# Seeding PSUM banks from ScalarE: D times xc, the mixer's residual and the convolution's last tap

## The reference

```python
xb, z = split(rms_norm(x) @ in_proj_w)
xc = silu(conv1d(xb, conv_w, 4 taps, causal, per channel) + conv_b)
dt, B, C = split(xc @ x_proj_w); dt = softplus(dt @ dt_proj_w + dt_proj_b)
h = exp(dt * A) * h + dt * B * xc          # a scan over the 1024 tokens
y = sum over states of h * C
y = (y + xc * D) * silu(z)
out = y @ out_proj_w + x                   # residual
```

## Time and profile before

| | us |
|---|---|
| median of 3 runs | 2755.98 (2751.46 to 2756.31) |
| the profiled execution's own time | 2754.25 |
| its span, first to last instruction | 2752.5 |
| busy: PE | 2418.8 |
| busy: DVE | 2434.5 |
| busy: ACT | 1633.1 |
| busy: POOL | 1511.1 |

### The profile page before, as it was taken

How to read it: one execution, slowest core, us unless ns; L and a number is a source line. 1 busy time by engine, 2 the same in 40 slices (tenths; PEclk the granted TensorE clock), 3 DMA queues, 4 the chain that set the end, 5 groups by cost and what they waited for, 6 DMA issues and landing times.

```text
span 2752.5 us, 27115 instructions
## 1 busy us (share of the span) xinstructions
PE 2418.8 (88%) x8416; PEld 1183.5 (43%) x8416; DVE 2434.5 (88%) x3233; ACT 1633.1 (59%) x3312; POOL 1511.1 (55%) x548
## 2 busy tenths in 40 slices
PE   4556799998989999998999999898999989888987
PEld 1112254453545444444544445453544545443554
DVE  1699999999999999999999999999999999999532
ACT  3565656666665667566566667666566666644321
POOL 0255565655556565655656565565656555565422
PEclk9777899999999999999999999999999999999999
DMA  1623253534344343524435353443535343442232
GB/s 35 231 86 124 94 177 93 180 118 153 114 134 155 118 158 118 183 87 156 140 115 177 101 176 109 144 137 103 186 93 179 118 155 105 137 157 80 68 87 56
DMA packets 175563, 353.43 MB, mean 128 GB/s; under 512 B 16283, under 2 KB 82108, under 8 KB 166972
## 3 DMA queue, kind: packets, MB, share of 16 engines
q1 hardware_dynamic: 164668, 334.93, 36.3%
q0 software_dynamic: 10752, 16.78, 3.7%
HBM read 291.35 MB, written 51.90 MB: 125 GB/s over the span
## 4 chain that ended last, share of the span: by engine, by line
DVE 57%; issue 19%; ACT 15%; PE 7%; POOL 1%; DMA 1%; DVEq 0%; SPq 0%; POOLq 0%; ACTq 0%
DVE hs L897 26%; DVE hs L883 12%; DVE th L1007 5%; DVE th L1012 4%; ACT DX L529 2%; DVE XC L856 2%; PE Gp L424 2%; ACT dA L511 1%; ACT L511 1%; PE Up L432 1%; PE FP L351 1%; PE FP L361 1%; ACT XC L582 1%; ACT SZ L587 1%; ACT XB L529 1%
## 5 line engine op out<-in xcount | busy, mean ns | idle before, releaser
L782 POOL TENSOR_TENSOR hs<-hs,Cb 128x2048 f32<-128x2048 f32 x256 | 1170.6, 4572 | 199.8 <-DVE hs L883 199.8
L511 ACT ACTIVATE dA<-dtr,A 128x512 f32<-128x512 f32 x1024 | 701.8, 690 | 827.9 <-DVE hs L897 826.9
L762 POOL TENSOR_TENSOR th<-th,cmb 128x512 f32<-128x512 f32 x256 | 338.1, 1325 | 803.4 <-DVE hs L883 711.8
L897 DVE TENSOR_TENSOR_SCAN hs<-dA,carry,hs 128x512 f32<-128x512 f32 x512 | 627.7, 1265 | 19.8 <-ACT dA L511 19.4
L424 PE MATMUL Gp<-x2T,Wgu 128*128 128x512 f32 x1024 | 532.6, 645 | 115.2 <-DVE th L1007 115.1
L897 DVE TENSOR_TENSOR_SCAN hs<-dA,hs 128x512 f32<-128x512 f32 x512 | 596.1, 1203 | 31.6 <-ACT dA L511 31.1
L883 DVE TENSOR_TENSOR hs<-dxr,Bb 128x2048 f32<-128x2048 f32 x256 | 601.9, 2351 | 12.5 <-DMA dxr<-dx_d 12.5
L432 PE MATMUL Up<-x2T,Wgu 128*128 128x512 f32 x1024 | 492.7, 604 | 0.0
L442 PE MATMUL MY<-Wdn,th 128*128 128x256 f32 x2048 | 486.4, 380 | 0.2 <-POOL th L762 0.2
L442 PEld LDWEIGHTS MY<-Wdn,th 128*128 128x128 f32 x2048 | 383.5, 190 | 137.4 <-issue 94.7
L424 PEld LDWEIGHTS Gp<-x2T,Wgu 128*128 128x128 f32 x1024 | 182.2, 196 | 449.5 <-issue 253.6
(11 more groups left out here) (131 smaller groups left out, 1820.5 us busy)
## 6 DMA issues: line engine op xcount, KB each, us to landing
dtr<-dt_d SPq DMA_DIRECT2D x64, 1024.0 KB, 5.7
dxr<-dx_d SPq DMA_DIRECT2D x128, 512.0 KB, 7.5
cmb<-cm_d SPq DMA_DIRECT2D x256, 256.0 KB, 3.7
Wdn<-in_w_dn SPq DMA_DIRECT2D x256, 128.0 KB, 3.6
dt_d<-XB SPq DMA_DIRECT2D x16, 1024.0 KB, 4.3
dx_d<-DX SPq DMA_DIRECT2D x16, 1024.0 KB, 5.9
Bb<-bc_d SPq DMA_DIRECT2D x64, 256.0 KB, 3.0
Cb<-bc_d SPq DMA_DIRECT2D x64, 256.0 KB, 4.0
```

Of the source, the lines that this page charges most:

```text
L511: act.activation(dA[h % 2][:, :], dtr[:, M % 2, beta, :], ACT.Exp, scale=A[:, k:k + 1]).then_inc(s_dA, 1)
L762: pool.tensor_tensor(th[:, q % NTH, :], th[:, q % NTH, :], cmb[:, q % 2, :], ALU.mult).then_inc(m_a, 1)
L782: pool.tensor_tensor(hs[:, G % NH, :, :], hs[:, G % NH, :, :], Cb[:, s, :].unsqueeze(1).broadcast_to([P, NBETA, CH]), ALU.mult).then_inc(s ...
L897: dve.tensor_tensor_scan(hv, dA[h % 2][:, :], hv, first, ALU.mult, ALU.add).then_inc(s_h, 1)
```

## The change

ACT writes three addends into the PSUM banks before PE adds its products:

- `y_begin`, new, heads ACT's groups g = 2, 6, 10, 14. It waits for `silu_x` and `y_gate` and writes D times xc into `Y` (new semaphore `y_seed`). `add_states` waits for `y_seed`; its `Ddiag` matmul is gone.
- After `f_b` of blocks 2 and 3, ACT rewrites `FP` in place as last tap times value plus bias (steps `seed2`, `seed3`). `f_conv` adds three taps to it without a bank of its own; `f_tap` becomes a plain copy.
- `p_xn` writes into `FP`, not `rn`, and moves: half 0 to the end of g = 1, half 1 to g = 3 behind `p_rev(0)`. `p_out` adds onto it. The identity matmul is gone. At stages without a front (p = 15, 16) a matmul `p_clear` (fill `rz`, g = 1) comes first. One matmul into `Y` (`y_first`) is added at the start of the program.

The rows of `Y` are now in natural channel order, so the stores permute the channels: each of the two 1 MB stores becomes four of 32 partitions each. The setup no longer builds `Ddiag` (4 DVE instructions) and builds 6 of 8 blocks of `Kdiag`.

```diff
-FREED_BY = dict(..., b2='raw2', b3='raw3', k2='tap2', k3='tap3', ...)
+FREED_BY = dict(rz='xn0', ..., k2='tap2', k3='tap3', ...)
...
-        def channels(t, c):
-            return t.rearrange('(c m p) t -> c p m t', m=MT, p=P)[c]
+        def channels(t, c, b):
+            return t.rearrange('(c m k b) t -> c b k m t', m=MT, k=CB, b=NBETA)[c, b]
...
-                        sp.dma_start(channels(dt_d, c), dt).then_inc(st_dt, 16)
+                        for b in range(NBETA):
+                            sp.dma_start(channels(dt_d, c, b), dt[b * CB:(b + 1) * CB, :, :]).then_inc(st_dt, 16)
...
             pe.wait_ge(w_dve, 2)
+            pe.matmul(Y[:, :], ident, Win[:, 0, 0:CH], start=True, stop=True).then_inc(y_first, 1)
...
             def f_conv(p, m):
-                bank_free(p, f'k{m}')
-                pe.wait_ge(f_act.sem, f_act.at(c, f'raw{m}'))
+                pe.wait_ge(f_act.sem, f_act.at(c, f'seed{m}'))
...
-                for k in range(TAPS):
+                for k in range(HIST):
...
+            def p_clear(p):
+                bank_free(p, 'rz')
+                pe.matmul(FP[:, :], ident, Win[:, 0, 0:CH], start=True, stop=True).then_inc(fp_full, 1)
...
             def p_out(p, k):
-                bank_free(p, f'r{k}')
+                pe.wait_ge(p_act.sem, p_act.at(c, f'xn{k}'))
...
-                    mm = pe.matmul(o, ident, rn[:, b, :], start=False, stop=True)
...
             def add_states(G):
                 if s == 0:
-                    if G > 0:
-                        pe.wait_ge(y_gate, G // NSIG)
-                    pe.wait_ge(f_act.sem, f_act.at(c, 'silu_x'))
-                    pe.matmul(Y[:, :], Ddiag[:, m, :], XC[:, c % 2, m, :], start=True, stop=False)
+                    pe.wait_ge(y_seed, G // NSIG + 1)
...
             def f_b(p, m):
                 act.activation(XB[:, m, HIST:], FP[:, :], ACT.Copy).then_inc(f_act.sem, 1)
+                if m in PE_CONV:
+                    act.activation(FP[:, :], FP[:, :], ACT.Identity, scale=conv_w[:, m, HIST:HIST + 1], bias=conv_b[:, m:m + 1]).then_inc(f_act.sem, 1)
...
+            def y_begin(M):
+                c, m = divmod(M, MT)
+                act.wait_ge(f_act.sem, f_act.at(c, 'silu_x'))
+                if M > 0:
+                    act.wait_ge(y_gate, M)
+                else:
+                    act.wait_ge(y_first, 1)
+                act.activation(Y[:, :], XC[:, c % 2, m, :], ACT.Identity, scale=d_col[:, m:m + 1]).then_inc(y_seed, 1)
...
             for p, g, G in groups():
+                if 0 <= G - 2 < NGRP and g % NSIG == 2:
+                    y_begin((G - 2) // NSIG)
                 if 0 <= p < NC:
                     decay(G * NBETA + 2)
                     decay(G * NBETA + 3)
                 if R_ and g in (3, 4):
                     p_rev(p, g - 3)
+                if R_ and g == 3:
+                    p_xn(p, 1)
...
-                if R_ and g in (0, 1):
-                    p_xn(p, g)
+                if R_ and g == 1:
+                    p_xn(p, 0)
```

More of the change, by code:

```diff
@@ L53, in fills_of @@
 def fills_of(p):
-    return [f for f in FILLS if (in_e(p) if f in E_FILLS else in_p(p) if f in P_FILLS else in_f(p))]
+    return [f for f in FILLS if not (f == 'rz' and in_f(p)) and (in_e(p) if f in E_FILLS else in_p(p) if f in P_FILLS else in_f(p))]
 FILL_NO = {pf: k for k, pf in enumerate([(p, f) for p in range(-2, NC + 1) for f in fills_of(p)])}
@@ L107, in sandwich_kernel @@
         A = sb('A', [P, GPC * NBETA])
-        Ddiag = sb('Ddiag', [P, MT, P])
-        Kdiag = sb('Kdiag', [P, len(PE_CONV) * TAPS, P])
+        Kdiag = sb('Kdiag', [P, len(PE_CONV) * HIST, P])
         Ebias = sb('Ebias', [P, TB * NE])
-        Cst = sb('Cst', [P, P + CB + NG * NG + TB * NE + P])
+        Cst = sb('Cst', [P, P + CB + NG * NG + TB * NE])
         SelDt = sb('SelDt', [2 * NS + 1, P])
@@ L168, in sandwich_kernel @@
         e_act = Steps(sem('e_act'), ['sum', 'nm', 'sq', 'xr'])
-        f_act = Steps(sem('f_act'), ['xT0', 'xT1', 'raw0', 'tap0', 'raw1', 'tap1', 'raw2', 'tap2', 'raw3', 'tap3', 'z0', 'silu_x', 'xd', 'dt', 'z1', 'z2', 'z3', 'silu_z'])
+        f_act = Steps(sem('f_act'), ['xT0', 'xT1', 'raw0', 'tap0', 'raw1', 'tap1', 'raw2', 'seed2', 'tap2', 'raw3', 'seed3', 'tap3', 'z0', 'silu_x', 'xd', 'dt', 'z1', 'z2', 'z3', 'silu_z'])
         f_dve = Steps(sem('f_dve'), [f'c{k}{m}' for m in DVE_CONV for k in range(HIST)] + ['hist', 'dx'])
@@ L172, in sandwich_kernel @@
         s_u, s_dA, s_h, s_keep, s_c, s_y, y_gate = (sem(k) for k in ('s_u', 's_dA', 's_h', 's_keep', 's_c', 's_y', 'y_gate'))
+        y_first, y_seed = (sem('y_first'), sem('y_seed'))
         route = ['den', 'score', 'sfc', 'ps', 't1', 't2', 'gs', 'ggt', 'geq', 'gq', 'ga', 'gr', 'gm', 'tmp', 'top', 'gt', 'eq', 'ng', 'cs', 'cn', 'ok', 'sel', 'w', 'ws', 'we', 'wr', 'comb']
         p_dve = Steps(sem('p_dve'), ['w1', 'nb', 'Bw1'] + rsqrt_names('q') + ['Bnb'] + route)
-        p_act = Steps(sem('p_act'), ['xn0', 'xn1', 'rev0', 'rev1', 'nm', 'sq', 'ro', 'sum2', 'nm2', 'sq2', 'x2', 'x2T0', 'x2T1', 'sig', 'cmT'])
+        p_act = Steps(sem('p_act'), ['xn0', 'rev0', 'xn1', 'rev1', 'nm', 'sq', 'ro', 'sum2', 'nm2', 'sq2', 'x2', 'x2T0', 'x2T1', 'sig', 'cmT'])
         m_g, m_u, m_d, m_th, m_v, m_w, m_a = (sem(k) for k in ('m_g', 'm_u', 'm_d', 'm_th', 'm_v', 'm_w', 'm_a'))
@@ L274, in _ @@
                         sp.wait_ge(f_act.sem, f_act.at(c, 'dt'))
-                        sp.dma_start(channels(dt_d, c), dt).then_inc(st_dt, 16)
+                        for b in range(NBETA):
+                            sp.dma_start(channels(dt_d, c, b), dt[b * CB:(b + 1) * CB, :, :]).then_inc(st_dt, 16)
                     if g == 11:
                         sp.wait_ge(f_dve.sem, f_dve.at(c, 'dx'))
-                        sp.dma_start(channels(dx_d, c), DX[:, :, :]).then_inc(st_dx, 16)
+                        for b in range(NBETA):
+                            sp.dma_start(channels(dx_d, c, b), DX[b * CB:(b + 1) * CB, :, :]).then_inc(st_dx, 16)
                 if in_p(p) and g == 10:
@@ L355, in f_conv @@
                 c = p + 1
-                bank_free(p, f'k{m}')
-                pe.wait_ge(f_act.sem, f_act.at(c, f'raw{m}'))
+                pe.wait_ge(f_act.sem, f_act.at(c, f'seed{m}'))
                 if m == PE_CONV[0] and c > 0:
                     pe.wait_ge(f_dve.sem, f_dve.at(c - 1, 'hist'))
-                for k in range(TAPS):
-                    mm = pe.matmul(FP[:, :], Kdiag[:, PE_CONV.index(m) * TAPS + k, :], XB[:, m, k:k + CH], start=k == 0, stop=k == TAPS - 1)
+                for k in range(HIST):
+                    mm = pe.matmul(FP[:, :], Kdiag[:, PE_CONV.index(m) * HIST + k, :], XB[:, m, k:k + CH], start=False, stop=k == HIST - 1, skip_group_check=True)
                 mm.then_inc(fp_full, 1)
@@ L474, in _ @@
                     f_dt(p)
+                if R_ and not F and g == 1:
+                    p_clear(p)
                 if R_ and g in (2, 3):
@@ L570, in f_tap @@
                     act.wait_ge(s_y, (c - 2) * GPC + m * NSIG + 1)
-                act.activation(XC[:, c % 2, m, :], FP[:, :], ACT.Identity, bias=conv_b[:, m:m + 1]).then_inc(f_act.sem, 1)
+                act.activation(XC[:, c % 2, m, :], FP[:, :], ACT.Copy).then_inc(f_act.sem, 1)
             def f_z(p, m):
@@ L613, in p_xn @@
                     act.wait_ge(e_dve.sem, e_dve.at(c, 'nbr'))
-                    act.wait_ge(st_dx, 16 * min(p + 1, NC))
+                    if in_f(p):
+                        act.wait_ge(f_act.sem, f_act.at(p + 1, 'tap2'))
+                    else:
+                        act.wait_ge(fp_full, filled(p, 'rz'))
+                else:
+                    act.wait_ge(p_act.sem, p_act.at(c, 'rev0'))
                 for b in (2 * k, 2 * k + 1):
-                    ins = act.activation(rn[:, b, :], x1[:, c % 2, b, :], ACT.Identity, scale=ln1[:, c, 0, b:b + 1], bias=ln1[:, c, 1, b:b + 1])
+                    ins = act.activation(FP[:, b % 2 * DM:(b % 2 + 1) * DM], x1[:, c % 2, b, :], ACT.Identity, scale=ln1[:, c, 0, b:b + 1], bias=ln1[:, c, 1, b:b + 1])
                 ins.then_inc(p_act.sem, 1)
@@ L800, in _ @@
                 dve.tensor_scalar(Win[:, q, :], Win[:, q, :], norm_w[:, q:q + 1], None, ALU.mult)
-            for m in range(MT):
-                dve.tensor_scalar(Ddiag[:, m, :], to_y, d_col[:, m:m + 1], None, ALU.mult)
             for m in PE_CONV:
-                for k in range(TAPS):
-                    dve.tensor_scalar(Kdiag[:, PE_CONV.index(m) * TAPS + k, :], ident, conv_w[:, m, k:k + 1], None, ALU.mult)
+                for k in range(HIST):
+                    dve.tensor_scalar(Kdiag[:, PE_CONV.index(m) * HIST + k, :], ident, conv_w[:, m, k:k + 1], None, ALU.mult)
             dve.memset(XB[:, :, 0:HIST], 0.0).then_inc(w_dve, 1)
```

33 lines of the change are left out of this document (15 added, 18 removed).

## The result

The changed kernel takes 2810.59 us (median; 2809.3 to 2812.08), the kernel before 2755.15 beside it: 1.0203 times as long, 95% interval 1.019 to 1.0217. The predicted time was 2808.

A forecast was written before the change was run, and what follows sets the result against it. The prediction took DVE, interrupted where ACT is late, to bound the steady stages. Wait 29 + clock 27 + 0.7 - 1.2 - 0.5 - 0.9 = +54 on 2754.25 gave 2808 us; range 2752 to 2842, 8 times in 10.

The forecast's parts named there:

- The wait: At g = 6 PE's sums wait for ACT's seed, so z0 and DVE's scan in g = 7 come 2.05 us later: 14 x 2.05 = 29 us.
- all but the wait and the clock: Seed at p = 0, setup, the head's convolutions and the tail: + 0.7 - 1.2 - 0.5 - 0.9 us.
- 2 us or more: Sign in the changed profile: ACT idle this long before f_z of z0 in g = 6, released by PE.
- The clock at g = 6: Behind a 3.8 us PE stall, gate and up run partly at 1.2 GHz, z0 2.1 us later: 13 x 2.1 = 27 us.
- The clock at g = 5: Rival: some 3 us idle before gate of g = 5 also brings 1.2 GHz; another 28 us, 2836 us; chance 0.13.
- The head's clock: Rival: y_first and the changed rhythm bring the clock up for the first projections; 7 us back, 2745 us; chance 0.13.
- The seed's own cost: On ACT, 0.65 us per seed of Y and 0.75 per FP; 96 seeds, about 66 us, beside idle time but for one place.
- PE's lighter work: PE loses 141 us, 6% of its work, all beside DVE's work; counted at nothing in the steady stages.
- The edits counted at nothing: y_begin at g = 2, 10, 14, seed2, seed3, the residual's half 1 and quartered stores: 0, but 0.7 at p = 0.
- The tail: At the program's end on PE, four identity pairs of 0.43 us go and p_clear adds 0.86: -0.9 us.
- The head and the rest: Setup without four Ddiag and two Kdiag instructions -1.2, the head's convolutions -0.5, tail -0.9, seed at p = 0 +0.7 us.

The follow-up runs named there:

- 2747.12: The changed kernel with the seed of Y ahead of f_tap at g = 5 and six matmuls of zeros before gate of g = 5: 2747.12 us, 0.9972.
- 2778.55: The changed kernel with matmuls of zeros in PE's idle time, seven before the sums of g = 6 and six before gate of g = 5: 2778.55 us, 1.0085.
- early-seed kernel: The changed kernel with y_begin of g = 6 moved on ACT to g = 5, ahead of f_tap: 2755.55 us, 0.9998 of before.

## Why the prediction was right

The time was right to 3 us, and in part by luck. The wait came as forecast. The clock cost 10 us less than forecast at g = 6 and some 15 more at g = 5, where the forecast had nothing; the start and the rest gave 5 us more than forecast, which hides that. The runs split the 56.3 us between 2754.25 and 2810.59 in three:

| part | runs | measured | forecast |
|---|---|---|---|
| all but the wait and the clock | 2747.12 - 2754.25 | -7.1 | -1.9 |
| `z0` late behind the seed | 2778.55 - 2747.12 | +31.4 | +29 |
| TensorE's clock | 2810.59 - 2778.55 | +32.0 | +27 |

The kernel before took 2754.69 and 2754.25 beside the filled kernels and 2755.15 beside the change, so the rows are good to about 2 us.

- *The wait.* Right in place, path and size. With both stalls filled the scan of g = 7 waits 3.02 and, in the other stages, 3.27 us against 0.86 and 0.98: 2.2 a stage, and 14 x 2.2 = 31. ACT's idle time before `f_z` is 3.18 us in the stage shown and the sums stall 3.47, against "2 us or more" and 3.8.
- *The clock at g = 6.* The mechanism held, the term was mis-sized: "13 x 2.1 = 27" assumed every stage. Ten of 13 are slow, by 6.2 - 4.53 = 1.7 us each: 17.
- *The clock at g = 5.* The prediction had it as a rival, with chance 0.13 and 28 us. It happened, in 11 of 13 stages, behind an idle time of 2.3 to 2.8 us; the earlier trace rows had shown 1.37 us without harm and 3.9 with it, and the forecast took the side between them that was wrong. So what happened is this rival, weaker than priced (2810.59 against its 2836), and not the forecast's picture of one slow place. It costs less than the rival's 2.0 a stage: 1.65 us at `gate` and `up`. The scan of g = 6 waits 1.5 to 1.8 us in these 11 stages, 18.6 in all; with both places filled, 0.52 in one. The 17 and these 18 make 35 of DVE's waits, which fall by as much with both filled (102.5 to 67.7); the time falls by 32. The two can't be priced one by one, for filling one moves part of the loss to the other. The rival's account of the idle time was wrong in part: with `Ddiag` back it stays, with convolution and residual back it goes.
- *The head's clock*, a rival that would have given 7 us back: `y_first` runs at 11.86 us in the change, and the first two projections after it take 3.75 and 3.78 us as before; it gave nothing there. In the profiled executions of six of the later kernels, one of them without `y_first` (`Ddiag` back), the second takes 1.98.
- *The seed's own cost* on ACT: 0.681 and 0.739 us against 0.65 and 0.75. As said, ACT's 57 us more lie beside idle time: the early-seed kernel has them too (1691.4 us busy) and takes 2755.55.
- *PE's lighter work*: no run shows a gain by it, as counted, and on the clock's side it costs. The Trainium skill's rule ("TensorE: Matmul & The Clock Gate", "HAM oscillation"), that a wait in each tile pays the warm-up again in each tile, holds in 21 of the change's 26 places, with idle times of 2.1 to 3.5 us; in five of them both products ran at 2.4 GHz.
- *The edits counted at nothing*: quartered stores 1.0002, without their permutation. The tail, forecast 0.9 us shorter, is as before to within 1 us.
- *The head and the rest*, forecast at -1.9 with setup, came to -7.1. In the profiled execution of the early-seed kernel with g = 5 filled, the first scan starts at 92.25 us instead of 97.13, 4.9 earlier, of which 1.4 lies in when the setup's load landed and 1.8 in the second projection, which takes 1.98 us there and 3.78 before. Both differ among the profiled executions of kernels that share this part of the program, so this is no sure gain of the edits. And DVE's `inputs`, 256 of them, are shorter:

```profile
L915 DVE TENSOR_TENSOR hs<-dxr,Bb 128x2048 f32<-128x2048 f32 x256 | 597.5, 2334 | 16.5 <-DMA dxr<-dx_d 16.5
```

Before they took 601.9 us in all, mean 2351 ns. Every kernel with the conv and residual seeds has 597.5 to 598.9, every one without them 600.3 to 602.1 (before, the seed of `Y` alone, the same with g = 6 filled, the quartered stores alone). What of these two edits frees DVE wasn't tried; 4 us hang on it.

## What to carry to other kernels

Moving an addend to another engine also moves its place in that engine's queue: the dear part was 0.68 us of work that ended 3.5 us after PE was free for it, 2 us later than PE had begun before, 14 times. Issuing it a few instructions earlier on ACT, ahead of `f_tap`, took the loss against the kernel before away. Before taking work off TensorE, look for where its idle time will be afterwards; idle time of 2.1 to 3.5 us ahead of products that someone waits for cost 0 to 3.0 us each in clock here. When two such stalls lie close to each other, price them together, since filling one alone can make the other longer.

## What the runs showed of the hardware

- The lower clock moves. The 3.47 us stall ahead of the sums of g = 6 is followed by 6.2 us in ten of 13 stages and by 4.53 in three in the change, where g = 5 is slow in 11. It is followed by 6.1 to 7.6 in 13 of 13 where g = 5 ran at 2.4 GHz throughout. The loss behind one stall is 0 to 3.0 us, not a constant. In the four kernels with the convolution and residual edits and no slow stretch at g = 6 (early seed, sums behind `up`, g = 6 filled, `Ddiag` back), g = 5 is slow in 6 or 7 of 13.
- Idle times of 0.4 to 1.1 us before `gate` at g = 5 never brought the lower clock (11 of 11 stages of the seed alone); 2.1 to 2.8 did in 11 of 13 stages of the change, 6 of 13 when g = 6 was filled.
- Six and seven small products of zeros a stage (each is two of the instructions shown), 2.9 and 3.2 us of PE work that no one waits for, are worth 32 us of the changed kernel's 2811. With `Ddiag` on PE the six alone take the ratio from 0.9982 to 0.9951.
- A ScalarE rewrite of a whole PSUM bank in place takes 0.739 us, a scaled write from SBUF into PSUM 0.681, and the next matmuls add onto both. In these kernels a matmul has written each bank before; no run leaves that out.
